# A table-gather attention layer with a weight-split FFN: another order of its start, its block loads and its adapter transfers

## The reference, cut to what matters

```python
# L0: attention over a paged cache. H=8 heads, G=4 key heads, HD=32, BLOCK=16, WINDOW=128
q, k, v = x @ Wq.T, x @ Wk.T, x @ Wv.T            # per head
q, k = rope(rms(q, q_norm_scale), pos), rope(rms(k, k_norm_scale), pos)   # pos = kv_lens + 0..31
blk = block_tables[b, pos // BLOCK]
k_blocks = k_blocks.at[blk, :, pos % BLOCK, :].set(k)     # new rows written into the blocks
v_blocks = v_blocks.at[blk, :, pos % BLOCK, :].set(v)
k_all, v_all = k_blocks[block_tables], v_blocks[block_tables]
scores = where(pos - WINDOW < kpos <= pos, q . k_all * SCALE, -inf)
x = x + (softmax(scores) @ v_all) @ Wo.T
# L1, L2: w1[cond[b]] and w2[subj[b]] are 32 x 32 matrices over the tokens; L2 adds side[subj[b]]
x = x + einsum('bct,bcd->bdt', x, w1[cond]);  x = x + einsum('bct,bcd->bdt', x, w2[subj]) + side[subj]
# L3: FFN of 256 -> 1024 -> 256, each product with a rank-16 adapter picked by subj[b]
h = silu(lora(x, Wg, Ag, Bg)) * lora(x, Wu, Au, Bu)
x = x + lora(h, Wd, Ad, Bd)                        # lora(x, W, A, B) = x W + (x A[subj]) B[subj]
```

## Time and profile before

| | us |
|---|---|
| median of 3 runs | 253.9 (253.25 to 255.11) |
| the profiled execution | 252.41 |
| its span, first to last instruction | 250.1 |
| PE busy | 207.7 (83%), 1995 matmuls |
| DVE busy | 143.0 (57%) |
| ACT busy | 105.2 (42%) |
| POOL busy | 70.4 (28%) |
| mean granted clock of TensorE | 0.965 of full |

### The profile page before, as it was taken

How to read it: one execution, slowest core, us unless ns; L and a number is a source line. 1 busy time by engine, 2 the same in 40 slices (tenths; PEclk the granted TensorE clock), 3 DMA queues, 4 the chain that set the end, 5 groups by cost and what they waited for, 6 DMA issues and landing times.

```text
span 250.1 us, 5105 instructions
## 1 busy us (share of the span) xinstructions
PE 207.7 (83%) x1995; PEld 187.9 (75%) x1995; DVE 143.0 (57%) x494; ACT 105.2 (42%) x291; POOL 70.4 (28%) x82
## 2 busy tenths in 40 slices
PE   2699978475865769959899799999979999899995
PEld 1577867364655658949789789888978988799994
DVE  5749878557656747285636644743664454326522
ACT  2163337656740573158323634632363463213310
POOL 3420047330038750176270443227040022000000
PEclk9999999859779999979999999999999999999999
DMA  6787899927983378899794012002200000010001
GB/s 167 219 173 110 187 190 239 320 73 160 136 222 93 105 182 120 195 202 190 130 156 111 3 42 66 0 3 73 76 1 3 0 3 0 3 42 3 0 3 42
DMA packets 64124, 25.25 MB, mean 101 GB/s; under 512 B 55780, under 2 KB 60836, under 8 KB 63524
## 3 DMA queue, kind: packets, MB, share of 16 engines
q1 hardware_dynamic: 60432, 14.07, 28.4%
q0 software_dynamic: 2944, 10.23, 16.1%
q10 hardware_dynamic: 724, 0.62, 0.8%
HBM read 17.83 MB, written 7.08 MB: 100 GB/s over the span
## 4 chain that ended last, share of the span: by engine, by line
PE 31%; issue 15%; DVE 13%; POOL 10%; DMA 5%; ACT 5%; SPq 4%; POOLq 1%
PE bank L1451 26%; POOL far L662 5%; SPq L542 4%; DMA early<-in_kb,blk_i 4%; POOL prob L676 3%; DVE prob L1084 3%; ACT prob L793 3%; DMA d_raw<-in_Wd 2%; DVE mask L1063 1%; PE bank L1437 1%; POOL near L665 1%; PE bank L1417 1%; POOL prob_near L677 1%; PE bank L1398 1%; DVE gs L1133 1%
## 5 line engine op out<-in xcount | busy, mean ns | idle before, releaser
L662 POOL DMA_INDIRECT far<-table_rows,place_i x32 | 31.5, 983 | 70.8 <-issue 37.2
L793 ACT ACTIVATE prob<-prob,ntop,qscale 128x160 f32<-128x160 f32 x64 | 32.4, 508 | 17.1 <-DVE ntop L1090 17.1
L1451 PE MATMUL bank<-xf_high,gu_high 128*128 128x256 f32 x128 | 39.1, 305 | 0.0
L1451 PE MATMUL bank<-xf_high,gu_low 128*128 128x256 f32 x128 | 36.3, 284 | 0.0
L1451 PE MATMUL bank<-xf_low,gu_high 128*128 128x256 f32 x128 | 36.3, 283 | 0.0
L1133 DVE SCALAR_TENSOR_TENSOR gs<-th,bank 128x256 f32<-128x256 f32 x32 | 13.4, 419 | 27.3 <-ACT th L828 27.0
L676 POOL TENSOR_TENSOR prob<-prob,rden 128x512 f32<-128x512 f32 x12 | 12.7, 1055 | 48.6 <-DVE rden L1109 48.6
L1451 PEld LDWEIGHTS bank<-xf_high,gu_high 128*128 128x128 f32 x128 | 24.6, 192 | 1.4 <-issue 1.0
L1451 PEld LDWEIGHTS bank<-xf_low,gu_high 128*128 128x128 f32 x128 | 24.5, 191 | 0.2
L1451 PEld LDWEIGHTS bank<-xf_high,gu_low 128*128 128x128 f32 x128 | 24.4, 191 | 0.0
L828 ACT ACTIVATE th<-bank 128x256 f32<-128x256 f32 x32 | 12.0, 380 | 24.3 <-PE bank L1451 24.3
(11 more groups left out here) (224 smaller groups left out, 523.2 us busy)
## 6 DMA issues: line engine op xcount, KB each, us to landing
table_rows<-early SPq DMA_DIRECT2D x32, 144.0 KB
table_rows<-far_probs SPq DMA_DIRECT2D x2, 512.0 KB, 3.6
gu_raw<-in_Wg SPq DMA_DIRECT2D x2, 512.0 KB, 5.2
gu_raw<-in_Wu SPq DMA_DIRECT2D x2, 512.0 KB, 5.7
d_raw<-in_Wd SPq DMA_DIRECT2D x2, 512.0 KB, 4.7
out<-xs SPq DMA_DIRECT2D x8, 128.0 KB, 1.9
xs<-in_x ACTq DMA_DIRECT2D x1, 512.0 KB, 5.0
xs<-in_x SPq DMA_DIRECT2D x1, 512.0 KB, 5.7
```

The costliest lines, as they stand in the source:

```text
L662: pool.indirect_dma_start(far[r][:, s, :], None, seen, bass.IndirectOffsetOnAxis(ap=far_i[:, GB * n + s:GB * n + s + 1], axis=0)).then_inc ...
L793: last = act.activation(v, v, ACT.Exp, bias=ntop[r][:, j:j + 1], scale=qscale[:, n, j:j + 1], accum_out=den[r][:, j:j + 1])
L1451: last = pe.matmul(dst, w[a], x[b], start=start and n == 0, stop=stop and n == 2)
```

## The change

1. The block numbers come first: VectorE computes the eight upper bits only and then the table shifts, makes `own_blk` for 9 instead of 11 slots, and TensorE turns them round as its first product. The rest (`wblk`, the lower bits, `len_f`, `four_len`, `diag_len`) follows, and VectorE waits a second time for TensorE (`slot_psum` 2).
2. The overwritten rows and their shifts (`moved_by`, `rows`) move behind the key products on VectorE, and TensorE's products on them behind three of the four projections of Q.
3. GpSimd no longer waits for the landing of groups 0 and 1 before `load_blocks(1)`. SP waits for it instead, ahead of b0, u0 and b1.
4. On SP, Wd moves ahead of scatter 2.
5. Ad's eight transfers and Bd's go from SP to GpSimd, behind `load_blocks(2)`.
6. In FIRST_ORDER, group 2's division goes from GpSimd to VectorE (norm0 behind first, norm1 behind up1, in place of den).

```diff
-BP = BT * SLOTS
+BP = BT * OLD
...
-     ("scores", 0), ("mask", 1), "gate1", ("first", 1), "up1", ("den", 0), ("prod", 1), "gate2", "up2",
+     ("scores", 0), ("mask", 1), "gate1", ("first", 1), ("norm0", 0), "up1", ("norm1", 0), ("prod", 1), "gate2", "up2",
...
@@ sync
             sp.wait_ge(zero_set, 2)
             mix_blocks()
+            for r in R:
+                sp.wait_ge(kv_in[r], 16 * (GB + 1))
             for a, src in enumerate((Bg, Bu)):
...
-            next_rows(2)
             sp.wait_ge(mixer_psum, 2)
             for half in range(2):
                 sp.dma_start(d_raw[:, half * half_d:(half + 1) * half_d].rearrange("p (k d) -> p k d", k=NF // 2),
...
-            sp.wait_ge(ssum_ready, SUMS)
-            for k in range(NF):
-                sp.dma_start(ad_raw[:, k * NR:(k + 1) * NR].rearrange("p (n r) -> p n r", r=RANK),
-                             Ad[:, k * P:(k + 1) * P, :].rearrange("n p r -> p n r")).then_inc(w_in["ad"], 16)
-            sp.dma_start(bd_raw[:, :], Bd.rearrange("n r f -> (n r) f")).then_inc(w_in["bd"], 16)
+            next_rows(2)
             next_rows(3)
@@ gpsimd
             for r in R:
                 prepare(r, r)
-            for r in R:
-                pool.wait_ge(kv_in[r], 16 * (GB + 1))
             load_blocks(1)
+
+            def load_adapter():
+                pool.wait_ge(ssum_ready, SUMS)
+                for k in range(NF):
+                    pool.dma_start(ad_raw[:, k * NR:(k + 1) * NR].rearrange("p (n r) -> p n r", r=RANK),
+                                 Ad[:, k * P:(k + 1) * P, :].rearrange("n p r -> p n r")).then_inc(w_in["ad"], 16)
+                pool.dma_start(bd_raw[:, :], Bd.rearrange("n r f -> (n r) f")).then_inc(w_in["bd"], 16)
...
                     if step[0] == "load":
                         load_blocks(step[1])
+                        if step[1] == 2:
+                            load_adapter()
@@ vector
-            for k in range(12):
+            for k in range(11, 3, -1):
                 dve.tensor_scalar(bits[:, k:k + 1], len_i[:, 0:1], k, 1, ALU.logical_shift_right, ALU.bitwise_and)
-            then(dve.tensor_scalar(len_i[:, 1:2], len_i[:, 0:1], BLOCK - 1, None, ALU.bitwise_and))
-            then(dve.tensor_copy(len_f[:, 0:2], len_i[:, 0:2]))
...
+            dve.tensor_tensor(own_blk[:, :, :], over(blk[:, 0:OLD], 2, BT), over(c3("eighth"), 1, OLD), ALU.mult
                               ).then_inc(slot_ready, 1)
...
+            k_products(0)
+            rope_table(1)
+            k_products(1)
+            k_finish(0)
+            k_products(2)
+            k_products(3)
+            k_finish(1)
             dve.wait_ge(rows_psum, 1)
             won, own = small("rows", B), c3("own")
             then(dve.scalar_tensor_tensor(moved_by[:, :], won, float(TILE_ROWS - 1), own, ALU.add, ALU.subtract))
...
             last.then_inc(shift_ready, 1)
-            k_products(0)
-            rope_table(1)
...
-            k_finish(1)
@@ tensor
+            pe.wait_ge(w_ready, 2)
+            project_q(0)
+            project_q(1)
+            project_q(2)
             pe.wait_ge(shift_ready, 1)
...
-            pe.wait_ge(w_ready, 2)
-            project_q(0)
-            project_q(1)
-            project_q(2)
             project_q(3)
```

More of the change, by code:

```diff
@@ L267, in build @@
         blk = sb("blk", [B, SLOTS])
-        own_blk = sb("own_blk", [B, SLOTS, BT])
+        own_blk = sb("own_blk", [B, OLD, BT])
         wblk = sb("wblk", [B, B, WS])
@@ L1210, in _ @@
             pe.wait_ge(ones_set, 1)
+            pe.wait_ge(slot_ready, 1)
+            pe.matmul(small("slots", BP), own_blk[:, :, :].rearrange("s j b -> s (j b)"), c3("tile"), start=True,
+                      stop=True).then_inc(slot_psum, 1)
             pe.wait_ge(pos_ready, 1)
+            pe.matmul(small("writer", NW)[:, 0:2], wblk[:, :, :].rearrange("s w n -> s (w n)"), ones[0:B, 0:2],
+                      start=True, stop=True)
             pe.matmul(small("writer", NW)[:, 2:4], c3("spread_writer"), len_f[:, 0:2], start=True, stop=True)
```

29 lines of the change are left out of this document (13 added, 16 removed).

## The result

The changed kernel is slower: 258.82 us as the median of 4 runs (256.79 to 259.74) beside 254.12 us for the kernel before on the same chip, a ratio of 1.019 with a 95% interval of 1.014 to 1.024. The forecast was 247.5 us with a range of 244.5 to 251.5. The profiled execution took 257.9 us, its span 256.0; before they were 252.4 and 250.1. The granted clock is 0.953 of full against 0.965. In all that follows a median is taken over every run of a kernel and a ratio only over the runs within 1.5% of its fastest, so where runs scatter (experiments 4, 5 and 12, whose profiled executions are among the slower ones) the ratio counts.

The account below looks back on a forecast made before the run. Bound ahead of 131 us by a chain of gathers, loads and scatters over three queues. Lead (how much earlier a step comes) 5.9 + 1.0 - 0.7 = 6.2 us; 253.9 - 6.2 = 247.7, say 247.5; range 244.5 to 251.5.

Parts of the forecast that it names:

- Step 1: Start: place-row work goes behind the key products; first gather at about 31.6 us, no second-transpose wait, lead 2.1 us.
- Step 2: Second block load at about 44.3 us, scatter from 52 to 54, third group's gathers at 65.5; lead 3.7 us.
- Step 3: Third group's softmax division on VectorE: TensorE's 1.32 us and a like wait go; lead 3.7 + 1.6 = 5.3 us.
- Step 4: d_raw loads ahead of the third scatter land by 91 us, ScalarE doesn't wait; lead 8.5 at fourth group's score rows.
- Step 5: GpSimd ahead of the fourth group's division: gathers at 101.1 us, GpSimd free at 110.0; lead falls to 5.9 us.
- the disputed one: Adapter's eight plain transfers issued by GpSimd behind the third load: 1.9 us each taken, done at 97.6 us, hidden.
- rival (a): GpSimd's descriptors cost by the piece: about 261 us at 4 us each, about 292 at 7.9; chance 0.12.
- MODIFY_POOL_CONFIG: Comes with GpSimd's first multiply, now unhidden at 110.0 us; price between 0 and 2.6 us, 0.7 taken.
- Rival (b): Lead spent ahead of the fourth group by MODIFY_POOL_CONFIG's 2.6 us and d_raw, scatter, adapter crowding: 251.5 to 254; chance 0.14.
- Rival (d): Start yields nothing, since second load and gathers meet in the DMA engines: 249.7 us; chance 0.62 together with the forecast.
- Rival (c): Scatter isn't slowed, code load is free, GpSimd's halves are quick: lead 8 to 9.5, 244.5 to 246 us; chance 0.12.

Follow-up runs that it names:

- experiment 4: Changed kernel with the adapter's nine GpSimd transfers moved ahead, behind the second block load instead of the third: 257.43 us, ratio 1.010.
- experiment 5: Changed kernel with the wait for the second group's gathers back on GpSimd ahead of the second block load: 258.67 us, ratio 1.015.
- experiment 12: Kernel of experiment 11 with the old order of the start put back, place-row work ahead of the key products: 249.11 us, ratio 0.976.
- experiment 11: Changed kernel, fourth group's division ahead of fifth group's gathers and fourth load, adapter on SP, SP's wait before b weights removed: 245.49 us, ratio 0.969.
- Experiment 8: Changed kernel with the third group's softmax division back on GpSimd: 258.01 us, ratio 1.016.
- experiment 1: Changed kernel with the adapter's nine transfers issued by SP again, behind the third scatter: 252.84 us, ratio 0.994.
- experiment 7: Changed kernel with both the adapter back on SP and Wd back behind the third tile's scatter: 251.53 us, ratio 0.989.
- experiment 6: Changed kernel with the two Wd loads back behind the third tile's scatter, adapter still on GpSimd: 254.26 us, ratio 1.005.
- experiment 9: Kernel before the change with only the adapter's nine transfers moved from SP to GpSimd, behind load_blocks(2): 259.96 us, ratio 1.021.

## Why the prediction was wrong, step by step

**What bounds the kernel** was read rightly: the time is made ahead of 131 us, and the chain of gathers, loads and scatters makes it. The error is in what I let the transfers cost each other.

**Step 1** (lead 2.1, first gather 31.6): right in mechanism, a little short in size. The gather started at 32.77; it was `place_i` that came last and no longer the new rows, so the moved work was not quite hidden. 1.0 us of that is this execution's later start of VectorE's work (rope_c at 18.86 against 17.87 us); counted from there the order gave 1.8 us. The second key transposes started at 50.96 with no wait: a lead of 1.1.

**Step 2** (lead 3.7, gathers at 65.5): here the prediction first fails by more than a microsecond. The second load went out at 45.34 and the scatter began at 53.05, as forecast. The sentence that failed is that holding the weights back "costs nothing" since they are wanted only behind 65 us. That looked at who waits for the weights and not at whom they stand beside. They met the scatter (the b weights landed 11.0 and 13.5 us after their issue, in place of 4.8 and 7.7; SP's queue moved 1.99 MB in the scatter's 13.5 us, before 0.95 MB in 8.6), it took 13.53 us, and the gathers started at 70.30, 4.8 us behind the forecast. TensorE's wait grew to 4.30 us in place of going; the lead was 1.1. Experiments 5 and 11 show the scatter at 8.7 and 8.6 us as soon as the weights are out before it, in 11 with the block load as early as in the changed kernel, so it isn't the load that slowed it.

**Step 3** (lead 5.3): the division on VectorE did what it should. TensorE's first transposes stand without a wait and the second with 0.49 us, where it had 1.32 and 0.88. The step itself gave what was forecast, 1.8 for 1.6: the lead rose from -0.5 at the second mixer products (88.44 against 87.93) to 1.3 at the value products (93.95 against 95.25). The missing 4.0 are 2.6 from steps 1 and 2 and 1.6 that the prediction had no term for, with the 0.2 gained here against them. TensorE stood 4.30 us ahead of the third key transposes and worked behind them at a granted clock of 0.53 until 84 us (before 1.00): the transposes took 1.12 us for 0.66, the scores 1.87 for 1.36, and the lead of 1.1 became -0.5. Experiment 8, with the adapter in front of the division on GpSimd, makes the step worth over 4 us to TensorE in this kernel and nothing to the time.

**Step 4** (lead 8.5): ScalarE no longer waits for Wd, and the lead rose by 3.2, as forecast, to 4.5. But its loads took 10.4 us to land in place of 4.7, and, as experiments 1 and 7 show, they cost the scatter behind them 3 us (4 with the adapter there, experiment 6). I had priced that at nothing.

**Step 5** (lead 5.9): GpSimd was to be free at 110.0 and was at 121.0. The 11.0 us are, in order: 4.5 from the scatter's start (91.49 against 87.0, since the third load, inherited from step 2, was late); 6.2 from its length (16.45 against 10.24); nothing from the landing (3.9 as forecast); 0.3 from gathers and load (9.2 against 8.87). I had taken 1 us for "the adapter's small pieces in the same DMA engines" and nothing for Wd; they cost 3 to 4 each. This is the larger of the two terms that failed: overlap in the DMA engines taken at 1 us, measured 7.1 (9.37 to 16.45).

The price that I had called the disputed one was the wrong one to dispute. The eight adapter rows of GpSimd took 0.95 us each (1.9 taken, 1.06 the bound of transport) and with Bd's ended at 94.07, 17.7 us ahead of the gathers: rival (a) falls. MODIFY_POOL_CONFIG, for which I took 0.7 us, showed 0.1 at most: the fourth load ends at 120.99 and the multiply starts at 121.10. The rule of the Trainium skill, GPSIMD Engine Reference, 2.1 Instruction dispatch, that the first call to freshly loaded code pays about 6 us more, isn't seen here either. Whether MODIFY_POOL_CONFIG loaded any code in this kernel, no row shows.

**The rivals.** Rival (b) named the crowding of Wd, scatter and adapter, with gathers at 103 to 105 us and 251.5 to 254 us. That is the mechanism; its size was a third of the measured one, gathers at 111.8, and it got 0.14. That the forecast called it at worst no change, and put the slower side on the price of GpSimd's descriptors alone, was the error in the chances. The trace of before had a bound. Its view of the DMA queues over the third scatter (92.4 to 101.6 us) and over the adapter on SP (103.4 to 111.8 us) reads:

```profile
q1 hardware_dynamic: 7396, 0.94, 73.6%
q0 software_dynamic: 34, 0.18, 7.2%
...
q1 hardware_dynamic: 7315, 1.45, 91.3%
q0 software_dynamic: 161, 0.46, 18.2%
```

The scatter's stretch has the 16 engines taken for 81% of its time, and the adapter's (with Wd and some gathers in it) for all of its 8.4 us; its shares add up to 109.5%, so they are no exact measure of how full the engines are. Two such stretches laid over each other left little room for 9.24 + 1. An estimate from these rows would have run from 9.24 to some 16 us, 9.24 plus the 6.6 by which the other stretch's 8.4 exceed the scatter's free fifth, 1.8, and the slower side would have had a case of its own. Rival (d) is not what the changed kernel shows: gathers and second load met and the second transposes didn't wait. With the weights there too (experiment 11) they waited 1.76 us. Rival (c) had the free code load right and the scatter wrong.

**The sum.** Forecast lead 6.2, measured -5.2 at the division (121.10 against 115.86), and -6.3 at the fifth group's transposes (it was -4.9 when TensorE came out of its 9.61 us; from there to the value products, at the lower clock, it took 7.5 us for 6.1); -5.9 in the spans and -4.7 in the medians.

## What to carry to other kernels

When a transfer is moved, ask not only who waits for it and how long its issue takes, but which transfers run at the hour it will run, and whether one of those is what the next step waits for. Here a run of small pieces that took three quarters of the DMA engines' time had no room beside it, and each newcomer lengthened it by 3 to 4 us, about its own work: start from that sum, full size, and not from nothing. And when an in-order queue (here GpSimd's) holds a step whose data are ready behind a step that waits for transfers, look at that order first: here it made the kernel proof against the crowd and was worth 10.5 us on the changed kernel. In the kernel before it would have been worth little, since there GpSimd was free 1.46 us ahead of that division and waited for VectorE; it became worth something by the rest of the change.

## What the runs showed of the hardware that I had not expected

- A plain transfer issued by GpSimd cost it 0.95 us for 1024 pieces of 64 bytes and 0.55 us for 128 pieces of 512 bytes, so some 0.45 ns a piece more. SP took 0.74 to 1.06 us for the same.
- On the profile's count, moving the adapter took 8464 packets from SP's queue (60432 to 51968) and gave GpSimd's 304 (2944 to 3248): so it counts some 28 pieces as one. The work did not shrink with the count. From experiment 1 to the changed kernel, where nothing else moves, the packets' time in 16 engines fell by 5.1 us in SP's queue (29.4% of 249.9 us to 26.7% of 256.0) and rose by 4.3 in GpSimd's (16.5% to 17.8%).
- The landing of one 512 KB weight transfer went from 4.6 us (the first b_raw in experiment 5) to 10.4 us (Wd in the changed kernel) and 17.2 us (the slower b_raw in experiment 4), with more running beside it each time.
- MODIFY_POOL_CONFIG ahead of GpSimd's first multiply cost 0.1 us or less in each place where nothing hid it (at 121.0 us in the changed kernel, at 94.1 us in experiment 8, at 99.1 us in experiment 9).
- After a pause of 9.61 us TensorE's granted clock was 0.50 from 120 to 128 us, and after one of 4.30 us 0.53 from 79 to 84 us. Behind the pause of 2.59 us in the kernel before it was 1.00 from 80 to 84 us, but behind one of 2.21 us in experiment 6 it was 0.66 from 79 to 84, so the length of the pause alone doesn't tell.
